# Expert tiles scattered as fp16 high and low parts and loaded by a transposing DMA, with three sets of banks and buffers and the first layer two tiles ahead

## The chip, the cores and the metric

The kernel runs on 1 core of a Trainium2 chip. The core has five engines that work side by side: TensorE (PE, matrix products), VectorE (DVE), ScalarE (ACT), GpSimd (POOL) and SyncE (SP, which here only issues DMAs). The metric is the device time of one execution in microseconds (us), here the median of 3 runs.

## The reference, cut to what matters

The program is a gated two-layer block over 32 sequences of 128 tokens with 256 features. The second part of the second layer is a mixture of 8 experts of which each token takes 2, and it is this part that the change touches:

```python
x2 = layernorm(x).reshape(T, 256)              # T = 32 * 128 = 4096 tokens
logits = x2 @ router_w                         # 8 experts
probs = softmax(logits); top_p, top_e = top_k(probs, 2)
for each of the 2 * 4096 (token, expert e) rows:
    h = gelu(x2[row] @ w_in[e] + b_in[e])      # 256 x 256
    y = (h @ w_out[e] + b_out[e]) * top_p
out = x + tanh(g_ffn[1]) * (sum of a token's two y)
```

## The kernel before, in words

**Stage 1, pairs of sequences.** 16 pairs (p = 0 to 15) go through the first layer, the attention and the router. All engines work on several pairs at once in an order written out by hand, one list of calls for each engine. At the end of a pair its attention output is added (`make_x3`), normalised ("E": `statistics_e`, `means`, `variances` on DVE, `inverse_root("E", p)` on POOL, `shifts` on DVE), and ACT writes the normalised rows twice (once for each choice) into `xn_e`, with the number of the output row in column 256 (`normed_e`, `output_rows`). PE transposes them for the router (`transpose_e`), DVE picks experts and finds each row's place (`slots`), and POOL scatters the rows with four indirect DMAs of 128 rows (`scatter`, line 765) into `store_x` in HBM, where the rows of one expert lie together. A row is 257 float32.

**Stage 2, tiles of 256 rows.** `store_x` is read back in 39 tiles (i = 0 to 38), each of one expert. SP issues `load_block(i)` (line 525), 257 KB, into one of five buffers `xb` (later 14). PE transposes a tile with four 128x128 products (`transpose_block`, line 1826) into PSUM. ACT copies it as fp16 (`copy_hi`), DVE writes the rest that fp16 lost (`copy_lo`). The first layer is 12 products (`layer1`: high by high, high by low and low by high, two halves), then ACT applies the gelu and makes the high part of the hidden values (`gelu`, `hidden_hi`), DVE the low part (`hidden_lo`). The second layer is 12 more products (`layer2`), DVE adds the bias into `y_out` (`add_bias`), and POOL scatters the two halves of the tile into `store_y` (`keep_block`, line 771, 128 rows of 1 KB each). `y_out` has five buffers. DVE's `take_rows(i)` writes the scatter's row numbers and waits until the scatter of tile i - 5 has landed. Between the two scatters of a tile POOL raises a 128x2 array to a power (`long_pause`, line 778), up to tile 35. PE's order is transposition of tile i, first layer of i - 1, second layer of i - 2. Banks and buffers of the hidden values come in two sets.

**Stage 3, sums.** SP loads the two outputs of each token (`load_outputs`), DVE adds them with the gates to x (`add_pair`), partly beside the last tiles. The last pairs need the last tile.

Each engine works strictly in the order of its list, and so does SP's queue. Around the handover from stage 1 to 2 SP's list reads: load tile 0, load tile 1, `keep_parts("q", 15)` (store the last pair's queries to scratch), `stack_queries(15)` (eight loads of them), then the other tiles. The scores of pair 15 on PE wait for these.

## Time and profile before

| | |
|---|---|
| runs | 472.47, 473.06, 476.50 us (median 473.06) |
| profiled execution | 474.49 us, of it 472.6 us span of the trace |
| busy PE / DVE / ACT / POOL | 394.9 / 368.8 / 331.4 / 268.7 us |
| DMA | 87.10 MB, mean 184 GB/s |

The profile lists for each engine how long it was busy, for groups of instructions how long the engine stood idle before them and what ended that wait, and the chain of work that ended last. Busy PE is not PE at its peak, since products overlap; the spacing of their starts tells the pace. A busy share is a mean over stages that have different bounds, so the stages are looked at one by one.

### The profile page before, as it was taken

How to read it: one execution, taken by the hardware profiler on the slowest of the kernel's cores; microseconds unless marked ns; L12 is line 12 of the kernel's file. 1: busy time of each engine (PE TensorE's matmuls, PEld its weight loads, DVE VectorE, ACT ScalarE, POOL GpSimd, SP SyncE). 2: the span in 40 equal slices, each digit the busy share in tenths (PEclk: the TensorE clock that was granted, in tenths of full speed). 3: DMA queues.
4: the chain of work that ended last, by engine and by line, in shares of the span. 5: the costliest groups of instructions: out<-in, count | busy, mean ns of one | idle time of the engine just before them, and what ended most of it. 6: DMA issues, size and time to landing. Idle time of an engine off the chain costs nothing.

```text
span 472.6 us, 13099 instructions
## 1 busy us (share of the span) xinstructions
PE 394.9 (84%) x4092; PEld 308.3 (65%) x4092; DVE 368.8 (78%) x1416; ACT 331.4 (70%) x671; POOL 268.7 (57%) x313
## 2 busy tenths in 40 slices
PE   2758899998999989999899987789559999979850
PEld 1536667776776777677686765568438897967740
DVE  2888888998988889899789786367655667779994
ACT  2855788898889889898879877566706666646640
POOL 2522112545454364626545565769988888888870
PEclk9998999999999999999999999899959999999996
DMA  7245576664565555875553774624335569396985
GB/s 242 83 139 163 180 214 179 196 181 141 177 213 170 166 171 167 221 204 184 180 174 111 223 220 121 198 68 130 101 126 143 170 175 332 116 341 251 323 275 204
DMA packets 69500, 87.10 MB, mean 184 GB/s; under 512 B 9485, under 2 KB 55290, under 8 KB 69306
## 3 DMA queue, kind: packets, MB, share of 16 engines
q1 hardware_dynamic: 60074, 65.81, 46.7%
q0 software_dynamic: 6816, 18.65, 10.8%
q10 hardware_dynamic: 2544, 1.81, 1.2%
q8 instruction: 35, 0.57, 0.5%
q14 instruction: 31, 0.25, 0.2%
HBM read 51.07 MB, written 35.18 MB: 182 GB/s over the span
## 4 chain that ended last, share of the span: by engine, by line
PE 42%; POOL 17%; issue 14%; DVE 10%; DMA 8%; ACT 6%; ACTq 0%; POOLq 0%; DVEq 0%; SPq 0%
PE ps_J L1650 12%; PE ps_F L1650 6%; POOL store_y L771 6%; DMA store_y<-y_out,y_row 6%; PE ps_O L1764 5%; PE ps_T L1659 5%; POOL store_x L765 5%; PE ps_S L1751 5%; POOL pause_t L778 5%; PE ps_R L1689 2%; PE ps_O L1775 2%; PE ps_G L1650 2%; DMA temp_t<-in_temp 1%; DVE y_out L2934 1%; DVE xb_lo L2903 1%
## 5 line engine op out<-in xcount | busy, mean ns | idle before, releaser
L771 POOL DMA_INDIRECT store_y<-y_out,y_row x78 | 81.4, 1044 | 21.8 <-issue 16.5
L765 POOL DMA_INDIRECT store_x<-xn_E,slot_u x64 | 68.0, 1063 | 26.5 <-DVE slot_u L2633 13.6
L1089 ACT ACTIVATE prob<-ps_S 128x512 f32<-128x512 f32 x128 | 72.4, 594 | 12.7 <-PE ps_S L1751 10.0
L778 POOL TENSOR_TENSOR pause_t<-half_ones,minus_half 128x2 f32<-128x2 f32 x71 | 54.7, 770 | 1.9
L1751 PE MATMUL ps_S<-q_stack,k_stack 128*128 128x256 f16 x256 | 44.5, 276 | 5.9 <-issue 3.8
L2922 DVE TENSOR_TENSOR h_lo<-h_f,h_hi 128x512 f16<-128x512 f32 x39 | 26.9, 689 | 21.0 <-ACT h_hi L1173 9.4
L1650 PE MATMUL ps_J<-wout_hi,h_hi 128*128 x112 | 31.2, 278 | 14.3 <-DVE y_out L2934 10.9
L1764 PE MATMUL ps_O<-prob,v_wide 128*32 128x128 f32 x1024 | 41.0, 279 | 1.1 <-ACT prob L1089 0.5
L1165 ACT ACTIVATE h_f<-ps_F,bin_t 128x256 f32<-128x256 f32 x56 | 23.4, 470 | 24.5 <-PE ps_F L1650 18.9
L751 POOL TENSOR_TENSOR rstd_C<-var_C,minus_half 128x2 f32<-128x2 f32 x16 | 12.1, 759 | 40.4 <-DVE var_C L2412 40.4
L1650 PE MATMUL ps_F<-xb_hi,win_hi 128*128 128x256 f16 x112 | 31.7, 283 | 3.9 <-DVE xb_lo L2903 3.3
L1751 PEld LDWEIGHTS ps_S<-q_stack,k_stack 128*128 128x128 f16 x256 | 21.7, 98 | 17.3 <-issue 10.4
L1775 PE MATMUL ps_O<-wo_t,av 128*128 128x256 f32 x128 | 31.2, 387 | 1.9 <-ACT av L1117 1.5
L1764 PEld LDWEIGHTS ps_O<-prob,v_wide 128*32 128x32 f32 x1024 | 24.2, 109 | 12.3 <-issue 10.2
L1650 PE MATMUL ps_F<-xb_lo,win_hi 128*128 128x256 f16 x112 | 31.6, 283 | 0.0
L1650 PE MATMUL ps_F<-xb_hi,win_lo 128*128 128x256 f16 x112 | 31.5, 281 | 0.0
L1650 PE MATMUL ps_J<-wout_hi,h_lo 128*128 x112 | 31.1, 278 | 0.0
L1650 PE MATMUL ps_J<-wout_lo,h_hi 128*128 x112 | 31.1, 278 | 0.0
L1152 ACT ACTIVATE xb_hi<-ps_R 128x512 f16<-128x512 f32 x28 | 16.6, 594 | 19.6 <-PE ps_R L1826 15.9
L751 POOL TENSOR_TENSOR rstd_E<-var_E,minus_half 128x2 f32<-128x2 f32 x16 | 11.8, 737 | 31.0 <-DVE var_E L2412 30.8
L756 POOL TENSOR_TENSOR inv_norm<-norm2c,minus_half 128x2 f32<-128x2 f32 x16 | 11.1, 694 | 32.2 <-DVE norm2c L2481 32.2
L1775 PEld LDWEIGHTS ps_O<-wo_t,av 128*128 128x128 f32 x128 | 23.1, 190 | 6.8 <-ACT av L1117 3.5
(301 smaller groups left out, 1399.5 us busy)
## 6 DMA issues: line engine op xcount, KB each, us to landing
parts_scratch<-parts SPq DMA_DIRECT2D x32, 256.0 KB
k_stack<-parts_scratch SPq DMA_DIRECT2D x64, 128.0 KB
q_stack<-parts_scratch SPq DMA_DIRECT2D x128, 64.0 KB
xb<-store_x SPq DMA_DIRECT2D x30, 257.0 KB
y_got<-store_y SPq DMA_DIRECT2D x14, 512.0 KB
c_in<-in_ctx SPq DMA_DIRECT2D x16, 256.0 KB
x_in<-in_x SPq DMA_DIRECT2D x16, 256.0 KB
store_x<-zeros SPq DMA_DIRECT2D x15, 257.0 KB, 4.6
```

Of the source, the lines that this page charges most:

```text
L751: pool.tensor_tensor(rstd[k][q][:, :], var[k][q][:, :], minus_half[:, 0:2], ALU.pow)\
L765: pool.indirect_dma_start(store_x, bass.IndirectOffsetOnAxis(slot_u[q][:, at:at + 1], 0), xn_e[q][:, at, :], None).then_inc(s_scat[q], 16)
L771: pool.indirect_dma_start(store_y, bass.IndirectOffsetOnAxis(y_row[n][:, b:b + 1], 0), y_out[n][:, b, :], None).then_inc(s_y_kept[n], 16)
L778: pool.tensor_tensor(pause_t[:, :], half_ones[:, :], minus_half[:, 0:2], ALU.pow).then_inc(s_set_p, 1)
L1089: act.activation(prob[m % PROBS][:, 2 * n:2 * n + 2, :, :], bank_s[n], ACT.Sigmoid, scale=float(HD) ** -0.5).then_inc(s_prob[n], 1)
L1165: act.activation(h_f32[q][:, m, :], hid_banks[side(i)][:, m, :], ACT.Gelu_apprx_tanh, bias=biases[:, bass.ds(at + m, 1)]).then_inc(s_gelu, 1)
L1650: ins = pe.matmul(o, l, r, start=start and i == 0, stop=stop and i == len(seq) - 1, skip_group_check=skip)
L1659: ins = pe.transpose(bank_t[:, i, b, :], src[:, b, 128 * i:128 * i + 128], ident[:, :])
L1751: ins = pe.matmul(bank_s[n][:, g % 2, :, :], k_stack[q][:, g, k, cut], q_stack[q][:, :, g, k, cut], start=True, stop=True)
L1764: ins = pe.matmul(bank_av[32 * g:32 * g + 32, k, b, :], v_wide[q][:, b, 4 * k + g, 2 * h:2 * h + 2, :].rearrange("p a d -> p (a d)"), prob ...
L1775: ins = pe.matmul(bank_o[:, b, :], av[:, k, b, :], wo_t[:, k, :], start=(k == 0), stop=(k == KT - 1))
L2922: dve.tensor_tensor(h_lo[q][:, :, :], h_f32[q][:, :, :], h_hi[q][:, :, :], ALU.subtract) .then_inc(s_h_lo, 1)
```

## The change

**Rows.** The row in `store_x` keeps its 1,028 bytes, but the first 1,024 now hold the 256 values as fp16 high parts and then as fp16 low parts. ACT writes the high parts (`rows_hi`, same two activations as before but fp16 out). DVE computes the normalised rows once in float32 into a separate array `xn_f` (`normed_e`, two instructions of 128x256 for each pair). POOL subtracts the one from the other and writes the low parts (`rows_lo`, one instruction of 128x1024 for each pair). `scatter(p)` waits for it. `transpose_e` reads `xn_f`.

**Tiles.** `load_block` issues a transposing DMA of 256 rows by 512 fp16 values, and a second DMA for the row numbers (256 pieces of 8 bytes). The first layer reads the landed tile directly: `transpose_block`, `copy_hi` and `copy_lo` are gone. A tile's buffer comes free after its first layer.

**Sets.** The hidden values and their PSUM banks, and the banks of the second layer, come in three sets instead of two (`HB = 3`); the first layer runs two tiles ahead of the second. The other loops are now written out as lists with the same content.

```diff
+            def rows_lo(p):
+                pool.wait_ge(s_rows_hi, 2 * p + 2)
+                pool.wait_ge(s_xn["E"], 2 * p + 2)
+                pool.tensor_tensor(e_lo[p % 2], xn_f[:, :, :].unsqueeze(2).broadcast_to([128, 2, TOP, D]), e_hi[p % 2],
+                                   ALU.subtract).then_inc(s_rows_lo, 1)
...
+            def normed_e(p):
...
+                for b in range(2):
+                    dve.tensor_scalar(xn_f[:, b, :], xs[:, 2 * p + b, :], mv["E"][q][:, b, 0:1], rstd["E"][q][:, b:b + 1],
+                                      ALU.subtract, ALU.mult).then_inc(s_xn["E"], 1)
...
-                    sp.wait_ge(s_xb_t, j + 1)
+                    sp.wait_ge(s_h, j + 1)
                     sp.wait_ge(s_y_row, j + 1)
-                sp.dma_start(xb[n][:, :, :], store_x[bass.ds(row_at(i, 0), BLK), :]
-                             .rearrange("(p b) c -> p b c", b=SUB))\
-                    .then_inc(s_xb[n] if n < XB else s_late[(n - XB) // GROUP], 16)
+                at, done = row_at(i, 0), s_xb[n] if n < XB else s_late[(n - XB) // GROUP]
+                sp.dma_start(xb[n][:, :, :], store_x16[bass.ds(at, BLK), 0:2 * D], transpose=True).then_inc(done, 16)
+                sp.dma_start(row_no[n][:, :, :], store_x[bass.ds(at, BLK), D - 1:WIDE].rearrange("(b p) c -> p b c", b=SUB))\
+                    .then_inc(done, 16)
...
-                pe.wait_ge(s_xb_lo, i + 1)
+                    loaded(pe, i)
...
-                               [(xb_hi[q][:, k, :], xb_lo[q][:, k, :]) for k in range(KT)])
+                               [(tile[:, k, :], tile[:, KT + k, :]) for k in range(KT)])
...
-        hid_banks = [P[n][:, :].rearrange("p (k s) -> p k s", k=KT) for n in ("F", "S0")]
-        y_banks = [P[n][:, :].rearrange("p (b d) -> p b d", b=SUB) for n in ("J", "S1")]
+        hid_banks = [P[n][:, :].rearrange("p (k s) -> p k s", k=KT) for n in ("F", "S0", "R")]
+        y_banks = [P[n][:, :].rearrange("p (b d) -> p b d", b=SUB) for n in ("J", "S1", "O")]
```

Three places where instructions move. First SP's list at the handover, before the change. `xb` is a tile, `parts_scratch` the stored queries, `q_stack` their eight loads.

```order
127 L525 DMA xb<-store_x 128x514
128 L525 ISA
129 L525 DMA xb<-store_x 128x514
130 L476 DMA parts_scratch<-parts 128x2x512
131 L499 DMA q_stack<-parts_scratch 16x4x512 x8
```

And after it.

```order
127 L533 DMA_TRANSPOSE xb<-store_x 128x4x256
128 L534 ISA
129 L534 DMA row_no<-store_x 128x2x2
130 L533 ISA
131 L533 DMA_TRANSPOSE xb<-store_x 128x4x256
132 L534 ISA
133 L534 DMA row_no<-store_x 128x2x2
134 L483 DMA parts_scratch<-parts 128x2x512
135 L506 DMA q_stack<-parts_scratch 16x4x512 x8
```

Four issues instead of two, two of them transposing, now stand ahead of the store of the queries.

Second, POOL's list where the first tiles' scatters meet the last pair's, before the change (`store_y` is a tile's scatter, `store_x` a pair's, `pause_t` the pause).

```order
199 L771 DMA store_y<-y_out,y_row 28160x256
200 L778 TENSOR_TENSOR pause_t<-half_ones,minus_half 128x2
201 L765 DMA store_x<-xn_E,slot_u 36608x257
202 L778 TENSOR_TENSOR pause_t<-half_ones,minus_half 128x2
203 L765 DMA store_x<-xn_E,slot_u 36608x257
```

And after it.

```order
214 L846 DMA store_y<-y_out,y_row 28160x256
215 L857 TENSOR_TENSOR pause_t<-half_ones,minus_half 128x2
216 L829 TENSOR_TENSOR xn_E<-w_f,xn_E 128x4x256
217 L840 DMA store_x<-xn_E,slot_u 36608x257
218 L857 TENSOR_TENSOR pause_t<-half_ones,minus_half 128x2
219 L840 DMA store_x<-xn_E,slot_u 36608x257
```

The subtraction (`rows_lo(15)`, printed with the names of the memory that it shares) is put between the pause and the pair's first scatter. All else keeps its place, the pauses too.

Third, DVE's list in the steady part of stage 2, before the change, one tile.

```order
1068 L2903 TENSOR_TENSOR xb_lo<-ps_R,xb_hi 128x512
1069 L2913 TENSOR_TENSOR y_row<-xb,left_rows 128x2
1070 L2922 TENSOR_TENSOR h_lo<-h_f,h_hi 128x512
1071 L2934 ISA
1072 L2934 TENSOR_TENSOR y_out<-ps_J,bout_t 128x512
```

And after it.

```order
1065 L3269 TENSOR_TENSOR y_row<-row_no,left_rows 128x2
1066 L3278 TENSOR_TENSOR h_lo<-h_f,h_hi 128x512
1067 L3290 ISA
1068 L3290 TENSOR_TENSOR y_out<-ps_J,bout_t 128x512
```

The tile's low part is gone, the other three instructions stay in their order.

## Rows read from the trace of the kernel before

**Rows 1.** Stretches of the span: us of each engine, granted clock, DMA share, GB/s.
```profile
54.00:290.00 236.00, 219.64 (x2597) 166.79 (x2589) 204.36 (x941) 201.56 (x421) 111.52 (x133) 1.00 0.61 181
341.00:461.00 120.00, 100.28 (x860) 85.11 (x860) 89.07 (x201) 64.80 (x127) 98.97 (x104) 0.96 0.67 222
461.00:472.60 11.60, 0.00 (x0) 0.00 (x0) 4.96 (x12) 0.00 (x0) 0.96 (x1) 0.60 0.59 205
```

**Rows 2.** Page part 4: the chain that ended last, by engine.
```profile
PE 42%; POOL 17%; issue 14%; DVE 10%; DMA 8%; ACT 6%; ACTq 0%; POOLq 0%; DVEq 0%; SPq 0%
```

**Rows 3.** POOL in order of time, tiles' scatters: start, us, instruction, idle before.
```profile
344.20 0.96 POOL L771 DMA_INDIRECT store_y<-y_out,y_row  x1 [0.30 <-issue]
345.18 0.73 POOL L778 TENSOR_TENSOR pause_t<-half_ones,minus_half 128x2 f32<-128x2 f32 x1
346.10 1.04 POOL L771 DMA_INDIRECT store_y<-y_out,y_row  x1 [0.19 <-issue]
347.44 0.96 POOL L771 DMA_INDIRECT store_y<-y_out,y_row  x1 [0.30 <-issue]
...
423.81 1.39 POOL L771 DMA_INDIRECT store_y<-y_out,y_row  x1 [0.20 <-issue]
...
461.11 0.96 POOL L771 DMA_INDIRECT store_y<-y_out,y_row  x1 [0.30 <-issue]
```

**Rows 4.** POOL in order of time at the handover.
```profile
310.13 1.04 POOL L765 DMA_INDIRECT store_x<-xn_E,slot_u  x1 [3.37 <-DVE slot_u L2633]
...
318.57 1.52 POOL L771 DMA_INDIRECT store_y<-y_out,y_row  x1 [0.19 <-issue]
...
340.87 1.04 POOL L771 DMA_INDIRECT store_y<-y_out,y_row  x1 [0.20 <-issue]
```

**Rows 5.** Waits from 300 us on: who for whom, us in all, times, longest.
```profile
DVE y_row L2913 <- DMA store_y<-y_out,y_row: 13.1, 8, 7.0
...
POOL store_y L771 <- DVE y_out L2934: 5.2, 11, 0.8
```

**Rows 6.** PE in order of time, one tile.
```profile
385.13 0.27 PE L1650 MATMUL ps_S<-xb_hi,win_hi 128*128 128x256 f16 x1
...
387.75 0.60 PE L1826 MATMUL ps_T<-ident,xb 128*128 128x128 f32 x4
388.18 0.27 PE L1650 MATMUL ps_F<-xb_hi,win_hi 128*128 128x256 f16 x1
```

**Rows 7.** Groups by shape: instruction, count, busy us, mean ns, idle before.
```profile
L784 POOL MEMSET v_wide<- 128x1024 f32 x2 | 1.9, 952 | 0.0
...
L2903 DVE TENSOR_TENSOR xb_lo<-ps_R,xb_hi 128x512 f16<-128x512 f32 x28 | 19.1, 682 | 1.4 <-ACT xb_hi L1152 1.4
...
L2403 DVE BATCH_NORM_STATS2 stats_E<-xs 128x6 f32<-128x256 f32 x32 | 11.9, 412 | 0.1
```

**Rows 8.** SP's queue in order of time at the handover: start, us of issuing.
```profile
287.39 0.94 SPq L525 DMA_DIRECT2D xb<-store_x  x2
288.44 0.38 SPq L476 DMA_DIRECT2D parts_scratch<-parts  x1
```

**Rows 9.** PE in order of time when pair 15's scores begin.
```profile
298.50 0.60 PE L1751 MATMUL ps_S<-q_stack,k_stack 128*128 128x256 f16 x4 [1.98 <-issue]
299.88 0.39 PE L1650 MATMUL ps_F<-xb_hi,win_hi 128*128 128x256 f16 x1 [0.78 <-DVE xb_lo L2903]
```

**Rows 10.** Page part 3: DMA queues, packets, MB, share of 16 engines.
```profile
q1 hardware_dynamic: 60074, 65.81, 46.7%
q0 software_dynamic: 6816, 18.65, 10.8%
```

**Rows 11.** Waits from 60 to 290 us.
```profile
PEld ps_T L1659 <- ACT xn_E L1026: 1.7, 2, 1.3
```

**Rows 12.** POOL in order of time, the inverse roots of pairs 1 and 14.
```profile
86.41 0.69 POOL L751 TENSOR_TENSOR rstd_E<-var_E,minus_half 128x2 f32<-128x2 f32 x1 [5.94 <-DVE var_E L2412]
...
298.08 0.72 POOL L751 TENSOR_TENSOR rstd_E<-var_E,minus_half 128x2 f32<-128x2 f32 x1 [1.40 <-DVE var_E L2412]
```

More of the change, by code:

```diff
@@ L955, in _ @@
             long_pause()
+            rows_lo(14)
             scatter(14, 3)
@@ L3218, in _ @@
             shifts("E", 1)
+            normed_e(1)
             squares(4)
@@ L3966, in _ @@
             add_bias(8)
[L3968 to L3982 removed]
+            take_rows(11)
```

767 lines of the change are left out of this document (606 added, 161 removed).

## The prediction, made before the changed kernel was run

> **What bounds the kernel now.** I read the stretches first. From 54 to 290 us (stage 1) PE is busy 219.64 of 236 us and DVE 204.36, that is 93% and 87%; POOL only 47% [rows 1]. From 341 to 461 us (stage 2) PE is at 84%, DVE at 74%, ACT at 54%, while POOL shows 98.97 of 120 us [rows 1]. By shares alone PE would be the bound of stage 2, so the order of time has to decide. On PE a tile's products start at 385.13, the transpositions of the next tile at 387.75 and the next tile's products at 388.18 [rows 6]: 24 products in 2.62 us (0.109 each) and 0.43 us for the transpositions, 3.05 us a tile. On POOL a tile is one scatter at 344.20, a pause, a second scatter at 346.10, and the next tile's at 347.44 [rows 3]: 3.24 us a tile, with gaps of 0.30 and 0.19 us that end by "issue", so in which nothing was waited for. 3.24 is more than 3.05. So POOL, not PE, sets the pace of stage 2, although its busy share counts the gaps as idle. The rest of the trace agrees. From the scatter at 344.20 (tile 4) to the last at 461.11 (tile 38) are 116.9 us. The floor is 32 tiles at 3.24, then five scatters without pauses at about 1.27: 110.0. Only 6.9 us are stalls or lengthened issues, such as the one of 1.39 us [rows 3]; waits for `y_out` are part of it, 5.2 us from 300 us on, where the ordinary 0.2 to 0.3 of each is counted in [rows 5]. The chain that ended last has 42% PE, from stage 1, and 17% POOL with 14% "issue", mostly POOL's gaps [rows 2]. Behind the last scatter 11.6 us of landing, loading and adding follow [rows 1], which the change leaves alone.
>
> At the handover POOL waits 3.37 us for the places of pair 14 until 310.13, and from there works through four scatters, the tiles 0 to 2, pair 15's four scatters and tile 3 at 340.87 [rows 4], without a wait that counts. So the end of the kernel hangs on three things: when pair 14's places come (310.1), what POOL has to do from there on, and its stalls.
>
> **The change, part by part.**
>
> *Taken off the tiles.* PE loses 0.43 us a tile [rows 6], DVE 0.68 us (`xb_lo`, [rows 7]), ACT a copy. With POOL at 3.24 us a tile this buys nothing by itself: PE goes from 3.05 to 2.62 us and waits more. What it can take away is part of the 6.9 us of stalls. The third set and the first layer two tiles ahead act in the same direction. But DVE's `take_rows` waits 13.1 us in all for tile scatters to land, up to 7.0 us at a time [rows 5], and these waits, which precede `add_bias` in DVE's order, do not depend on PE; and the issue of 1.39 us is not changed either. I take 3.0 us of the 6.9: −3.0, between 0 and −6.9.
>
> *First tile.* The first products of tile 0 waited 0.78 us for `xb_lo` [rows 9]; the landed tile is there by then: −0.8.
>
> *`rows_lo(15)`.* It stands in POOL's unbroken stretch, so it counts in full. No such instruction is in the trace. A POOL memset of the same 1,024 elements takes 0.95 us [rows 7], a bound from below since it only writes; two operands in and one out at that pace would be 2.86, my bound from above. I take the middle, +1.9. The Trainium skill (GPSIMD Engine Reference, Performance versus the Vector engine) measures a two-operand operation over 2,048 elements at 4,497 ns, by which 1,024 would be an estimate of 2.25 us, and the sum 0.35 us higher; no row of this trace shows it.
>
> *`rows_lo(0)` to `(14)`.* They stand where POOL waits: 3.37 us before pair 14's first scatter [rows 4], 5.94 and 1.40 us before inverse roots [rows 12]. Where the wait is shorter than 1.9 us the inverse root comes up to 0.5 to 2 us late, of which ACT's order has covered most. I count 0 for these. If the cover is gone, each costs up to 1.9.
>
> *`normed_e`.* 32 instructions of 128x256 on DVE. The nearest row is `stats_E` over the same elements at 0.412 us [rows 7]: 0.8 us a pair, 13.2 in all. A pair takes 16.3 us (298.08 − 86.41 over 13 pairs, [rows 12]), of which DVE works 87%, 14.1 us [rows 1]; it would work 14.9. Nothing of it shows if the idle 13% takes it, all 13.2 if none does. I take a quarter, +3.3. Against that PE no longer waits for ACT's `xn_E` (1.7 us in stage 1, [rows 11]), since DVE's rows are ready sooner. Together +1.6.
>
> *The handover on SP.* Two tile loads take 0.94 us to issue, and the store of the queries follows at 288.44 [rows 8]; pair 15's scores begin at 298.50 after a wait [rows 9], and pair 14's router and its places come behind them on PE. Four issues in place of two put the store back by at least 0.94 us. The tiles ahead in the queue may also take longer. By the hardware queue's mean a packet of 1,095 bytes takes 58.8 ns (46.7% of 16 x 472.6 us over 60,074), by the software queue's one of 2,736 bytes 119.8 ns [rows 10]. The line through both is 18 ns a packet and 0.037 ns a byte. A tile takes 0.86 us as a load at the queue's mean rate; as 1,024 pieces of 256 bytes, my estimate of what a transposition reads, 27.5 ns each on 16 engines, it would take 1.76. Two tiles make 1.8 us, of which I count half: +1.8 in all, between 0.9 and 5.
>
> Sum: −3.0 − 0.8 + 1.9 + 1.6 + 1.8 = +1.5 us on a span of 472.6, so 474.1, and an execution of 476.0 where this one took 474.49 (1.9 us lie outside the span). The runs' median is 473.06; +1.5 on it is 474.6.
>
> **The rivals.**
>
> *A: POOL stays the bound (as above).* Ends of the unknown terms: −6.9, −0.8, +1.0, −1.7, +0.9 give −7.5; 0, 0, +2.9, +13.2, +5 give +21. They will not all fall one way; I give this case 467 to 480. Chance 0.60.
>
> *B: the transposing load is slower than a tile's 3.24 us.* If pieces are written 32 bytes at a time, a tile is 8,192 pieces, which at 18 to 19 ns are 9.9 us on 16 engines [rows 10]. It decides from 3.24 us a tile on. At 5 us the 39 tiles issued from 287.4 land at 482 instead of before 435, and with the 20 to 30 us that follow a last load the end is near 510. Against it: nothing in the trace forces pieces that small. The Trainium skill (DMA: Bandwidth & Descriptors, Latency and other measured facts) measured 261 GB/s for transposing DMAs, an estimate of 1.0 us for 256 KB; by that case B is out, and no row here shows it. Chance 0.15.
>
> *C: stage 1 becomes bound by DVE.* If DVE stands still while POOL subtracts, a pair's DVE time is 14.1 + 0.8 + 1.9 = 16.8 us against 16.3: +0.5 for each of 15 pairs and the waits of an engine without slack, some +8 to +15, 481 to 488. It decides once DVE is held for more than 1.4 us a pair. For it speaks that POOL's issues lengthen from 1.04 to 1.39 us in the late stretch in which DVE adds outputs [rows 3], so the two engines do seem to disturb each other. The Trainium skill (SBUF — State Buffer, SBUF: two separate sides) has a rule for it: DVE with two operands in SBUF and POOL share an exclusive lock for the whole instruction; by that rule only such DVE work is held, about a third of it. Chance 0.12.
>
> *D: faster by more than 1%.* The mechanism is the stall on POOL: if all 6.9 us were waits that shorter DVE and PE work removes, and stage 1 hides its additions, −6.9 − 0.8 + 1.0 + 0.9 = −5.8, 467.3. It needs a gain of 4.7 us or more. A gain like PE's 0.43 us x 39 = 17 us is excluded as long as POOL needs 3.24 us a tile. Chance 0.13.
>
> **How the numbers follow.** The likeliest is A, 474.6. 1% is 4.7 us and about what a measurement can tell. Same (468.3 to 477.8): 0.45 of A's 0.60 and 0.02 of C's. Slower: 0.13 of A, 0.15 of B, 0.10 of C. Faster: 0.02 of A and 0.13 of D. The range 467 to 488 leaves out B and a small part of the others.
>
> **What would show it.** POOL's tile period stays at 3.24 to 3.4 us while PE's 24 products take 2.62 and PE idles more: right. `rows_lo` at 1 to 2.9 us, with pair 15's between scatters: right. The store of the queries on SP about 1 us later. I am wrong if PE waits for loads of tiles (B), if a pair takes over 16.8 us (C), or if POOL's period falls under 3.2 us.

## The result and the profile after

The changed kernel takes 511.61 us (median, 507.63 to 513.64), beside 473.15 of the kernel before on the same chip: 1.079 times the time, with an interval of 1.070 to 1.087. The prediction was 474.6, the range 467 to 488. Both were wrong, and so was the weight on "same". In e9 and in e12 one run each was over 1.5% above the fastest run of its kernel; these two are left out of the ratios below.

| | before | after |
|---|---|---|
| span of the profiled execution | 472.6 us | 511.8 us |
| busy PE / DVE | 394.9 / 368.8 us | 392.5 / 379.3 us |
| busy ACT / POOL | 331.4 / 268.7 us | 309.2 / 305.7 us |
| packets of the hardware queue | 60,074 | 106,250 |

The first lines are from the page of the kernel after, parts 1, 3 and 4. The chain that ended last was PE's for 42% [rows 2]; now it is POOL's for 31%, and DVE's share is 17% where it was 10%.

```profile
PE 392.5 (77%) x3936; PEld 298.5 (58%) x3936; DVE 379.3 (74%) x1409; ACT 309.2 (60%) x632; POOL 305.7 (60%) x329
...
q1 hardware_dynamic: 106250, 65.86, 49.7%
...
POOL 31%; PE 21%; DVE 17%; issue 17%; ACT 7%; DMA 6%; POOLq 1%; ACTq 0%; DVEq 0%; SPq 0%
```

The stretches of [rows 1] in the kernel after (us of PE, PE's weight loads, DVE, ACT, POOL, then the granted clock, DMA share, GB/s). In the same 236 us of stage 1 PE does 210.35 us of work where it did 219.64, while DVE shows more, 212.61 for 204.36, in fewer instructions (880 for 941). Part of that is the work of `normed_e`; the rest is instructions that take longer than they did. In the stretch of the tiles the granted clock is 0.91 where it was 0.96, but that is not what the tiles lose: in e5 and e6, whose tiles are as quick as before in the table below, it is 0.93 and 0.92.

```profile
54.00:290.00 236.00, 210.35 (x2404) 158.54 (x2407) 212.61 (x880) 188.61 (x393) 126.85 (x134) 0.98 0.57 168
...
341.00:461.00 120.00, 84.67 (x699) 68.47 (x698) 58.93 (x152) 47.21 (x94) 95.73 (x99) 0.91 0.71 162
```

**Where the time went.** POOL in order of time (start, us, instruction, idle before) has four landmarks, which answer to [rows 12], [rows 4] and the end of [rows 3]: pair 15's inverse root, the first scatter of tile 0, the first scatter of tile 3, the last scatter.

```profile
87.81 0.69 POOL L819 TENSOR_TENSOR rstd_E<-var_E,minus_half 128x2 f32<-128x2 f32 x1 [5.16 <-DVE var_E L2763]
...
344.46 0.72 POOL L819 TENSOR_TENSOR rstd_E<-var_E,minus_half 128x2 f32<-128x2 f32 x1
345.38 1.04 POOL L846 DMA_INDIRECT store_y<-y_out,y_row  x1 [0.20 <-issue]
...
374.13 1.04 POOL L846 DMA_INDIRECT store_y<-y_out,y_row  x1 [0.20 <-issue]
...
500.36 0.96 POOL L846 DMA_INDIRECT store_y<-y_out,y_row  x1 [0.30 <-issue]
```

In the kernel before pair 15's root starts at 317.65; the others are 318.57, 340.87 and 461.11. So the span can be cut into four parts (they add up but for the 0.92 us between pair 15's root and tile 0's first scatter, the same in every run), and the same four can be read in every experiment:

| us | pair 15's root | tile 0 to tile 3 | tile 3 to last | last to end | span |
|---|---|---|---|---|---|
| before | 317.65 | 22.30 | 120.24 | 11.5 | 472.6 |
| after | 344.46 (+26.8) | 28.75 (+6.5) | 126.23 (+6.0) | 11.4 | 511.8 |
| e1 subtraction small | 319.84 | 27.05 | 125.66 | 11.7 | 485.2 |
| e2 `normed_e` small | 338.94 | 28.72 | 126.47 | 11.8 | 506.8 |
| e3 both small | 319.42 | 26.88 | 126.05 | 11.6 | 484.9 |
| e4 subtraction on DVE | 337.97 | 27.23 | 126.50 | 11.8 | 504.4 |
| e5 plain load | 343.84 | 29.08 | 120.65 | 12.0 | 506.5 |
| e6 no pauses | 347.62 | 27.67 | 120.93 | 11.9 | 509.0 |
| e7 before, no pauses | 320.33 | 20.28 | 125.68 | 12.1 | 479.3 |
| e8 before, busy POOL | 329.21 | 23.79 | 121.37 | 12.2 | 487.5 |
| e9 outputs earlier | 345.77 | 28.54 | 122.78 | 12.7 | 510.7 |
| e10 queries first | 342.97 | 28.62 | 126.20 | 11.4 | 510.1 |
| e11 subtraction in four | 342.90 | 29.63 | 124.07 | 11.6 | 509.1 |
| e16 plain, transposition later | 342.46 | 24.36 | 121.33 | 11.7 | 500.8 |
| e17 plain, three mends | 337.77 | 24.63 | 121.96 | 11.8 | 497.1 |
| e18 as e17, subtraction small | 320.79 | 24.62 | 120.90 | 12.0 | 479.2 |

The 39.2 us are three losses at three places, 26.8 in stage 1, 6.5 at the handover and 6.0 in the steady tiles. The experiments find a main cause for each.

A column of one profiled execution also moves from run to run without a cause. Pair 15's root does so most: the edits of e6, e9 and e10 come into play only after it or beside it, and it is at 347.6, 345.8 and 343.0, where the changed kernel has 344.5; in e7 it is 2.7 us later than in the kernel before. So up to some 5 us in the first column mean nothing by themselves. The third column of these kernels without an edit in stage 2 (after, e1 to e4, e10) lies between 125.7 and 126.5. Verdicts on a whole kernel are taken from the ratios. The kernel before, timed beside each of the four groups of experiments, took 473.0, 476.9, 477.8 and 471.6 us, so only ratios compare between groups (e1 to e4, e5 to e8, e9 to e12, e16 to e18).

### The profile page after: what moved, and what is told of

Same layout as the page of the kernel before. It is cut to its first block, busy times and chain, and to the rows that moved or that the text cites. A ratio compares the mean times of both kernels' runs of the same rounds, so it can differ in the third digit from the quotient of the medians.

```text
span 511.8 us, 12756 instructions
## 1 busy us (share of the span) xinstructions
PE 392.5 (77%) x3936; PEld 298.5 (58%) x3936; DVE 379.3 (74%) x1409; ACT 309.2 (60%) x632; POOL 305.7 (60%) x329
## 3 DMA queue, kind: packets, MB, share of 16 engines
q1 hardware_dynamic: 106250, 65.86, 49.7%
## 4 chain that ended last, share of the span: by engine, by line
POOL 31%; PE 21%; DVE 17%; issue 17%; ACT 7%; DMA 6%; POOLq 1%; ACTq 0%; DVEq 0%; SPq 0%
POOL store_y L846 11%; POOL pause_t L857 8%; POOL store_x L840 7%; PE ps_J L1891 5%; PE ps_T L1900 3%; DMA store_y<-y_out,y_row 3%; PE ps_O L2005 2%; PE ps_F L1891 2%; POOL xn_E L829 2%; PE ps_S L1891 2%; DMA y_got<-store_y 2%; POOL rstd_E L819 1%; ACT xn_B L1218 1%; PE ps_S L1992 1%; PE ps_R L1930 1%
## 5 line engine op out<-in xcount | busy, mean ns | idle before, releaser
L846 POOL DMA_INDIRECT store_y<-y_out,y_row x78 | 83.7, 1073 | 28.4 <-issue 17.6
L1285 ACT ACTIVATE prob<-ps_S 128x512 f32<-128x512 f32 x128 | 72.4, 594 | 24.6 <-PE ps_S L1992 23.6
L840 POOL DMA_INDIRECT store_x<-xn_E,slot_u x64 | 69.2, 1081 | 29.8 <-DVE slot_u L2996 19.0
L1354 ACT ACTIVATE h_f<-ps_S,bin_t 128x256 f32<-128x256 f32 x26 | 10.9, 471 | 41.9 <-PE ps_S L1891 37.4
L829 POOL TENSOR_TENSOR xn_E<-w_f,xn_E 128x1024 f16<-128x1024 f32 x16 | 33.1, 2068 | 0.3
L819 POOL TENSOR_TENSOR rstd_C<-var_C,minus_half 128x2 f32<-128x2 f32 x16 | 12.2, 760 | 35.2 <-DVE var_C L2763 35.1
L2005 PEld LDWEIGHTS ps_O<-prob,v_wide 128*32 128x32 f32 x1024 | 24.6, 110 | 12.6 <-issue 9.3
L1891 PE MATMUL ps_S<-wout_hi,h_hi 128*128 x52 | 15.7, 302 | 19.4 <-DVE h_lo L3278 19.3
L1249 ACT ACTIVATE xn_E<-xs,shift_E,rstd_E 128x512 f16<-128x512 f32 x32 | 24.2, 808 | 9.9 <-DVE shift_E L2769 9.9
L3278 DVE TENSOR_TENSOR h_lo<-h_f,h_hi 128x512 f16<-128x512 f32 x39 | 26.8, 688 | 2.1 <-ACT h_hi L1362 2.1
L1354 ACT ACTIVATE h_f<-ps_R,bin_t 128x256 f32<-128x256 f32 x26 | 10.9, 470 | 28.9 <-PE ps_R L1891 27.1
L1362 ACT ACTIVATE h_hi<-h_f 128x512 f16<-128x512 f32 x39 | 24.6, 630 | 1.2
L1280 ACT ACTIVATE parts<-ps_J 128x512 f16<-128x512 f32 x32 | 19.0, 594 | 10.0 <-PE ps_J L1891 9.9
L819 POOL TENSOR_TENSOR rstd_E<-var_E,minus_half 128x2 f32<-128x2 f32 x16 | 11.8, 738 | 22.1 <-DVE var_E L2763 21.7
L2825 DVE TENSOR_TENSOR parts<-ps_J,parts 128x512 f16<-128x512 f32 x32 | 21.9, 684 | 4.2 <-ACT parts L1280 4.1
```

Source lines behind the costliest of these rows:

```text
L819: pool.tensor_tensor(rstd[k][q][:, :], var[k][q][:, :], minus_half[:, 0:2], ALU.pow)\
L829: pool.tensor_tensor(e_lo[p % 2], xn_f[:, :, :].unsqueeze(2).broadcast_to([128, 2, TOP, D]), e_hi[p % 2], ALU.subtract).then_inc(s_rows_lo, 1)
L840: pool.indirect_dma_start(store_x, bass.IndirectOffsetOnAxis(slot_u[q][:, at:at + 1], 0), xn_e[q][:, at, :], None).then_inc(s_scat[q], 16)
L846: pool.indirect_dma_start(store_y, bass.IndirectOffsetOnAxis(y_row[n][:, b:b + 1], 0), y_out[n][:, b, :], None).then_inc(s_y_kept[n], 16)
L1285: act.activation(prob[m % PROBS][:, 2 * n:2 * n + 2, :, :], bank_s[n], ACT.Sigmoid, scale=float(HD) ** -0.5).then_inc(s_prob[n], 1)
L1362: act.activation(h_hi[q][:, :, :], h_f32[q][:, :, :], ACT.Copy).then_inc(s_h_hi, 1)
```

## The experiments

The theories after the result. **H (hold):** DVE stands still while POOL subtracts, in far more cases than rival C had it. **W (work):** the additional work of `normed_e` on a nearly full DVE is the loss. **B:** the transposing load. **P (pace):** POOL's list in stage 2, pauses and all, is what everything waits for. Later: **S**, SP's issues come late, and **O**, an order on PE.

### e1, e2, e3: the two additions cut down, one by one and together

In e1 and e3 POOL subtracts one column, in e2 and e3 DVE normalises eight:

```diff
-pool.tensor_tensor(e_lo[p % 2], xn_f[:, :, :]..., e_hi[p % 2], ALU.subtract)
+pool.tensor_tensor(e_lo[p % 2][:, :, :, 0:1], xn_f[:, :, 0:1]..., e_hi[p % 2][:, :, :, 0:1], ALU.subtract)
...
-dve.tensor_scalar(xn_f[:, b, :], xs[:, 2 * p + b, :], ...)
+dve.tensor_scalar(xn_f[:, b, 0:8], xs[:, 2 * p + b, 0:8], ...)
```

> The changed kernel with POOL's rows_lo cut to 1 of 256 values per row (the low parts of the scattered rows stay zero, so they are left out of the result); all waits stay. Theory H (DVE is held while POOL's subtraction runs): in the changed kernel's trace DVE's picks take 594 ns instead of 187, var_E 553 instead of 173, the two at which the subtraction usually falls; all together some 1.7 us a pair. They go back to 187 and 173, the pair period falls from 18.1 us to about 16.9, and the kernel to about 490 us (15 pairs x 1.2 = 18, and 2 for the one subtraction in POOL's unbroken stretch). Rival W (DVE's own new work, 0.82 us a pair, is what slows stage 1): the period stays at 17.8 or more and the time above 503 us.

Measured: 487.95 us, ratio 1.031 (1.022 to 1.039).

> The changed kernel with DVE's normed_e cut to 8 of 256 values (the router and the low parts see wrong rows; this work is left out); rows_lo in full. Theory H: only 0.5 us of DVE work a pair goes, the stretched instructions stay at 594 and 553 ns, the period falls from 18.1 to 17.4 to 17.7, the kernel to 500 to 505 us. Rival W: the period goes back to 16.3 to 16.6 and the kernel to about 487 us.

Measured: 508.03 us, ratio 1.073 (1.065 to 1.081), slower than the 500 to 505 that H had said, though a pair takes 17.66 us, as said.

> Both cuts at once (low parts and float32 rows left out, all waits and places kept). Theories H and W both: the period is back at 16.3 to 16.5 us and stage 1 costs nothing, so the time is what is left of the loss outside stage 1: handover 4 us and stage 2 with its transposing loads 6 us over the kernel before, 483 to 487 us. If a third cause in stage 1 exists (the order PE waits in, or DMA), the period stays above 16.8 us and the time above 490.

Measured: 486.24 us, ratio 1.027 (1.020 to 1.035).

The subtraction costs 1.079 − 1.031, some 23 us. The work of `normed_e` costs some 3 us by e2 and 1.7 by e3 against e1, both inside the intervals. In e1 pair 15's root comes at 319.84, so 24.6 of the 26.8 us of stage 1 are back, at once. W is out.

How a subtraction on POOL gets at stage 1 is seen where DVE and POOL stand side by side in time. The kernel after, DVE in order of time at pair 14's statistics:

```profile
321.18 0.25 DVE L2759 BATCH_NORM_AGGREGATE mv_E<-stats_E 128x2 f32<-128x6 f32 x2
321.47 1.72 DVE L2763 TENSOR_SCALAR var_E<-mv_E 128x2 f32<-128x2 f32 x1
```

And POOL at the same time:

```profile
321.08 2.07 POOL L829 TENSOR_TENSOR xn_E<-w_f,xn_E 128x1024 f16<-128x1024 f32 x1
323.27 0.72 POOL L819 TENSOR_TENSOR rstd_E<-var_E,minus_half 128x2 f32<-128x2 f32 x1
```

`var_E`, two numbers per partition, 0.16 us elsewhere, begins at 321.47 and ends at 323.19; the subtraction ends at 323.15. The hold also falls on the instruction for which POOL's own next one waits.

How often does this happen? Between 54 and 290 us POOL subtracts 11 times, and in 9 of them one instruction of DVE is drawn out and does not end before the subtraction does: `x` twice, `picks` three times, `var_E` twice, `both` and `win_lo` once each. Together they take 17.1 us more than they take otherwise, 1.55 for each of the 11. The longest, DVE and then POOL:

```profile
210.98 3.13 DVE L3332 TENSOR_TENSOR win_lo<-w_stage,win_hi 128x512 f16<-128x512 f32 x1
```

```profile
211.47 2.07 POOL L829 TENSOR_TENSOR xn_E<-w_f,xn_E 128x1024 f16<-128x1024 f32 x1
```

The other two subtractions (at 101.48 and 155.67) ran beside statistics and instructions with an operand in PSUM, which kept their ordinary lengths (only a small `ln_gain` behind the first of them took 0.2 us more). The means of the groups show the same. DVE's groups by shape (count, busy us, mean ns, idle before), the kernel before:

```profile
L2448 DVE TENSOR_TENSOR x<-moved,x_in 128x512 f32<-128x512 f32 x12 | 8.1, 679 | 0.0
L2976 DVE TENSOR_TENSOR win_lo<-w_stage,win_hi 128x512 f16<-128x512 f32 x6 | 4.1, 683 | 0.0
L2412 DVE TENSOR_SCALAR var_E<-mv_E 128x2 f32<-128x2 f32 x14 | 2.4, 174 | 0.0
L2597 DVE TENSOR_TENSOR picks<-route,rindex 128x32 f32<-128x32 f32 x13 | 2.4, 186 | 0.1
L2611 DVE TENSOR_TENSOR both<-picks 128x16 f16<-128x16 f32 x13 | 2.2, 168 | 0.1
```

The kernel after:

```profile
L2799 DVE TENSOR_TENSOR x<-moved,x_in 128x512 f32<-128x512 f32 x12 | 10.6, 883 | 0.0
L2819 DVE TENSOR_SCALAR w_f<-xs,mv_E,rstd_E 128x256 f32<-128x256 f32 x24 | 8.8, 411 | 0.0
L2807 DVE TENSOR_TENSOR xt_lo_E<-ps_T,xt_hi_E 128x512 f16<-128x512 f32 x12 | 8.2, 683 | 2.0 <-issue 1.7 <-ACT xt_hi_E L1211 0.2
L2960 DVE TENSOR_TENSOR picks<-route,rindex 128x32 f32<-128x32 f32 x12 | 7.1, 594 | 0.1
L2763 DVE TENSOR_SCALAR var_E<-mv_E 128x2 f32<-128x2 f32 x12 | 6.6, 553 | 0.0
L3332 DVE TENSOR_TENSOR win_lo<-w_stage,win_hi 128x512 f16<-128x512 f32 x5 | 5.8, 1166 | 0.0
L2974 DVE TENSOR_TENSOR both<-picks 128x16 f16<-128x16 f32 x12 | 4.6, 381 | 0.0
```

And e1:

```profile
L2765 DVE TENSOR_SCALAR var_E<-mv_E 128x2 f32<-128x2 f32 x14 | 2.9, 206 | 0.0
L2962 DVE TENSOR_TENSOR picks<-route,rindex 128x32 f32<-128x32 f32 x13 | 2.4, 187 | 0.1
```

Five groups grew. Each has one instruction a pair (`win_lo` in 5 pairs of 12), and the means rose by 0.41 us for `picks`, 0.38 for `var_E`, 0.21 for `both`, 0.20 for `x`, 0.48 x 5/12 = 0.20 for `win_lo`. That is 1.40 us a pair, 68% of the 2.07 us of the subtraction (counted by subtractions it is the 1.55, 75%). `xt_lo_E`, which has one operand in PSUM (`ps_T`), did not grow, 0.683 us. The Trainium skill (SBUF — State Buffer, Who interferes with whom) has this rule: a DVE instruction with two inputs in SBUF and a GpSimd instruction that reads SBUF shut each other out, and so do GpSimd and a DVE instruction in one of the two-port modes that a `tensor_scalar` can enter; a DVE instruction with at most one SBUF input outside these modes is free; the one that starts first keeps the ports for its whole instruction. Which groups grew (`var_E`, the `tensor_scalar`, at 0.553 us for 0.174) and that `xt_lo_E` did not (0.683) agree with it. Who starts first agrees for 4 of the 9 only. The other 5, as `win_lo` above, began 0.25 to 0.60 us ahead of the subtraction and still lasted to its end.

What comes of it for the pace can be told from the roots of pair 1 and pair 14, 13 pairs apart: 16.28 us a pair before [rows 12], and (323.27 − 87.81) / 13 = 18.11 after, with pair 14's root at 323.27 in the rows of POOL above. By the same two roots a pair takes 16.25 us in e1 and 17.66 in e2. So `normed_e`'s 0.82 us alone cost nothing a pair (e1), the hold with hardly any of it 1.38 (e2), and on top of the hold `normed_e` costs another 0.45.

One rival is left. POOL's next inverse root stands directly behind the subtraction in its list, so it could be POOL's own 2 us, and not the hold, by which DVE is late. But then DVE would wait for the root. It does not. DVE's waits for it between 54 and 290 us, in the kernel before, after and in e8 below (us in all, times, longest):

```profile
DVE shift_E L2418 <- POOL rstd_E L751: 0.5, 1, 0.5
...
DVE shift_E L2769 <- POOL rstd_E L819: 0.4, 2, 0.2
...
DVE shift_E L2443 <- POOL rstd_E L752: 0.4, 2, 0.2
```

### e8: the hold alone, put into the kernel before

```diff
+pool.tensor_tensor(unread[...], zeros[...], zeros[...], ALU.subtract)   # 128x736, once a pair, where rows_lo stands
```

> The kernel before plus one idle subtraction of 128x736 float32 values for each pair on POOL, at the places where the changed kernel has rows_lo (about 1.5 us each; nothing reads its result, nothing on DVE is added). Theory H: DVE is held for most of it, picks and var_E lengthen by 0.3 us or more, the pair period rises from 16.3 to 16.9 to 17.4, and the kernel takes 483 to 490 us. Rival W: POOL had room, so 473 to 476 us.

Measured: ratio 1.029 (1.022 to 1.035), so +13.6 us on 473. DVE's groups by shape in e8, and POOL's instruction that holds them:

```profile
L2622 DVE TENSOR_TENSOR picks<-route,rindex 128x32 f32<-128x32 f32 x12 | 5.2, 432 | 0.1
L2437 DVE TENSOR_SCALAR var_E<-mv_E 128x2 f32<-128x2 f32 x13 | 5.0, 387 | 0.0
```

```profile
L764 POOL TENSOR_TENSOR unread<-zeros 128x736 f16<-128x736 f32 x12 | 17.0, 1418 | 0.3
```

Nothing reads what POOL writes here, and no other part of the change is in this kernel. 1.42 us a pair on POOL, on an engine that stands idle for half of stage 1 [rows 1], still slow the kernel; the root of pair 15 comes 11.6 us later. The first 11 of these subtractions behind 54 us hold the same nine DVE instructions as in the kernel after, for 10.8 us in all or 0.98 for each of the 11, and a pair takes 17.26 us in place of 16.28, which is 0.98 more. With the waits for the root as small as shown above, this shows H by itself. (`picks` and `var_E` grew by 0.25 and 0.21 on the mean, a little less than the 0.3 expected.)

### e4, e11: the same subtraction elsewhere, and in pieces

In e4 DVE does it (`rows_lo` as five calls after `normed_e` in DVE's list). In e11 POOL does it in four instructions:

```diff
+for b in range(2):
+    for k in range(TOP):
+        pool.tensor_tensor(e_lo[p % 2][:, b, k, :], xn_f[:, b, :], e_hi[p % 2][:, b, k, :], ALU.subtract)
```

> The changed kernel with the same subtraction on DVE (128x1024, five calls after normed_e in its list) instead of on POOL. Theory H: DVE gets 1.1 us of work a pair and loses 1.7 us of standing still, the period falls from 18.1 to about 17.5 and the kernel to 500 to 504 us although DVE does more. Rival W: more DVE work makes it slower, 520 us or more.

Measured: 505.39 us, ratio 1.068 (1.059 to 1.076), a little above the 500 to 504 expected. DVE takes 1.23 us for it (mean of 12), a pair takes 17.41 us, and the kernel is about 1% faster than with 2.07 us on POOL (the two intervals overlap). Adding work to DVE did not make the kernel slower, as W had it: 1.23 us of work of its own are no dearer here than being held for 1.40.

> The changed kernel, with POOL's subtraction of a pair cut into four of 128x256 with the same result. Theory W (DVE is kept out for the whole of one POOL instruction, and gets in between two): an instruction of DVE is held by 0.6 us at most and not by up to 1.6, and 5 to 15 us of the 39 come back, 497 to 507 us, though POOL itself takes longer for the pair (about 0.2 us for each further instruction, 2.7 against 2.07 us). Theory T (what DVE loses goes with the time in which POOL works, however it is cut): nothing comes back, and POOL's longer time makes it 512 to 520.

Measured: ratio 1.069 (1.066 to 1.073), some 4.5 us less than the 1.079 of the changed kernel, by the middles of the two intervals (they overlap slightly; that of e10, 1.079 in the same group, does not reach it). DVE's groups by shape in e11, and POOL's pieces:

```profile
L2765 DVE TENSOR_SCALAR var_E<-mv_E 128x2 f32<-128x2 f32 x12 | 8.6, 718 | 0.0
L2962 DVE TENSOR_TENSOR picks<-route,rindex 128x32 f32<-128x32 f32 x12 | 5.5, 454 | 0.1
L2976 DVE TENSOR_TENSOR both<-picks 128x16 f16<-128x16 f32 x12 | 2.4, 200 | 0.0
```

```profile
L831 POOL TENSOR_TENSOR xn_E<-w_f,xn_E 128x256 f16<-128x256 f32 x44 | 28.6, 682 | 0.3
```

Four pieces of 0.68 us take 2.5 us from the start of the first to the end of the last, in place of 2.07. `both` is nearly free again and `picks` is held less, but `var_E` more. In the order of time of e11, DVE and then POOL:

```profile
233.70 2.31 DVE L2765 TENSOR_SCALAR var_E<-mv_E 128x2 f32<-128x2 f32 x1
```

```profile
233.50 2.49 POOL L831 TENSOR_TENSOR xn_E<-w_f,xn_E 128x256 f16<-128x256 f32 x4
236.10 0.72 POOL L819 TENSOR_TENSOR rstd_E<-var_E,minus_half 128x2 f32<-128x2 f32 x1
```

`var_E` begins in the first of the four pieces and ends at 236.01, with the last. So the expectation that DVE gets in between two pieces, and is never held by more than 0.6, is wrong for this instruction; why the next piece goes first was not found. Cutting helps a little and does not cure. Where it helps is open: pair 15's root in e11 is no earlier than in e10 (342.9 and 343.0).

### e5: the load without its transposition

```diff
-sp.dma_start(xb[n][:, :, :], store_x16[bass.ds(at, BLK), 0:2 * D], transpose=True)
+sp.dma_start(xb[n]..., store_x16[bass.ds(at, BLK), 0:2 * D].rearrange("(p b) c -> p b c", b=SUB))
```

> The changed kernel with a plain load of the same bytes in place of the transposing one (256 KB, 128 partitions of 2 KB), so that the first layer multiplies untransposed rows; the row number load stays. Theory S (SP's queue is what stage 2 lost: a transposing load takes 1.23 us to issue against 0.33 to 0.47 for a plain one, so the last 14 loads take 31 us and the first output loads leave at 451 instead of 413): the first output loads leave 10 us or more earlier against the last tile scatter, POOL's stall of 4.1 us near tile 28 goes, the handover is 1.5 us shorter, and the kernel is 4 to 8 us faster, 504 to 508 us. Rival T (the transposition moves data slowly and the landing is what is late): DMA share in stage 2 falls clearly (0.71 to under 0.6) and the gain is over 10 us. Rival N: POOL hides all of it, 510 to 512 us.

Measured: ratio 1.069 (1.060 to 1.078). B's 510 us was near the measured time, but its mechanism is out. Stage 1 and the handover are as slow as with the transposition (343.84 and 29.08), and only the steady tiles lose 5.6 us of their excess. The plain load changes both the transfer and SP's time to issue it. e9 leaves the transfer as it is and gets 3.4 of the 5.6 back by SP's order alone; the other 2.1 are not told apart.

### e9: SP comes late to the outputs

SP in order of time in the kernel after, the last loads of tiles and the first of outputs (start, us of issuing):

```profile
449.19 1.23 SPq L533 DMA_TRANSPOSE xb<-store_x  x1
450.62 0.42 SPq L534 DMA_DIRECT2D row_no<-store_x  x1
451.23 3.10 SPq L546 DMA_DIRECT2D y_got<-store_y  x5
```

DVE and then POOL, a little later in the same kernel:

```profile
455.85 0.88 DVE L3306 SCALAR_TENSOR_TENSOR result<-y_got,gate_all,xs 128x256 f32<-128x256 f32 x2 [6.33 <-DMA y_got<-store_y]
```

```profile
459.07 0.96 POOL L846 DMA_INDIRECT store_y<-y_out,y_row  x1 [4.10 <-DVE y_out L3290]
```

A transposing load occupies SP for 1.23 us (0.55 in e5) and the row numbers for 0.42 more; with gaps a tile takes SP 2.0 us, and the last 14 loads (tiles 25 to 38) keep it at work almost without a gap from 419.8 to 451.0. The first outputs stand behind them; the kernel before issues these at 412.6. DVE waits 6.33 us for these with `y_out` of the next tile behind it, and POOL waits for that. In e9 they are issued ahead of the last three tiles:

```diff
             load_block(35)
+            load_outputs(0) ... load_outputs(4)
             load_block(36)
```

> The changed kernel with one edit on SP's queue: the first five loads of output rows (y_got) are issued after the load of tile 35 and not after that of tile 38. In the changed kernel DVE stands 6.33 us for the first y_got and POOL then 4.10 and 1.37 us for DVE's y_out, because SP, at 2.0 us a tile, comes to the output loads only at 451.2 us. Theory S (SP's issues are the reason of these waits): the waits go, and 3 to 5.5 us with them: 506 to 508.5 us where before is 473 and after 511.6. Rival (the tile that y_got waits for, or the landing of the scatters, is what is late): under 1 us, 510.5 to 512.

Measured: ratio 1.067 (1.063 to 1.072), about 5 us less than the changed kernel, and clear of e10 in the same group (1.074 to 1.084). The steady tiles take 122.78 us for 126.23; DVE's wait for the outputs falls from 6.3 to 2.8 us, and POOL's waits for `y_out` in the tiles from 6.3 to 3.7. The outputs leave only 2.6 us earlier (448.6 for 451.2). S holds for this place, though e12 below does not repeat the gain.

### e10: the queries' store ahead of the first tiles

```diff
+            keep_parts("q", 15)
             load_block(0)
             load_block(1)
-            keep_parts("q", 15)
             stack_queries(15)
```

> The changed kernel with one edit on SP's queue: the store of the last pair's queries is issued ahead of the loads of tiles 0 and 1, and not behind them. Theory S: the store goes 3.6 us earlier and the eight loads of the queries start about 2.3 us earlier, so that PE's wait for them (4.71 us) shrinks by as much; 1.5 to 2.5 us fall: 509 to 510. Rival: PE's later wait (4.61 us for the transposition of pair 15, whose rstd stands behind pair 14's scatters on POOL) swallows it: 511 to 512, no change.

Measured: ratio 1.079 (1.074 to 1.084), no change. The eight loads start at 316.38 and not at 318.31, but PE waits 4.62 us later on all the same, as the rival said. What the prediction had costed as the handover on SP is not what the handover loses.

### e16: the order on PE at the handover

PE in order of time in the kernel after, with the transposition of pair 15's rows and the second layer of tile 1 (`ps_S`) behind it:

```profile
346.12 1.12 PE L1900 MATMUL ps_T<-ident,w_f 128*128 128x128 f32 x4 [4.61 <-DVE w_f L2819]
...
349.59 0.42 PE L1891 MATMUL ps_S<-wout_hi,h_hi 128*128 x1
```

POOL, which waits for tile 1 and then for tile 2:

```profile
352.85 1.04 POOL L846 DMA_INDIRECT store_y<-y_out,y_row  x1 [3.60 <-DVE y_out L3290]
...
357.55 1.04 POOL L846 DMA_INDIRECT store_y<-y_out,y_row  x1 [0.92 <-DVE y_out L3290]
```

In the kernel before this transposition stood behind the second layer of tile 1 on PE, in the one after ahead of it. It needs DVE's rows, these POOL's root of pair 15, and the root stands behind pair 14's four scatters. So tile 1 now waits for pair 15. This order is measured on the kernel with the plain load only, not with the transposing one. e16 puts it back, on the kernel of e5, so its tiles stand wrongly as in e5:

```diff
-            transpose_e(("E", 14), 15)
             layer1(3, 0)
             layer1(3, 1)
             layer2(1, 0)
             layer2(1, 1)
+            transpose_e(("E", 14), 15)
-            logits(("rank", 14), 15)
             layer1(4, 0)
             layer1(4, 1)
+            logits(("rank", 14), 15)
```

> The kernel of e5 (changed kernel, tiles loaded without transposition, so that the columns of a tile stand wrongly and its output is not the reference's) with one edit on PE's list: the transposition of pair 15's rows for the router stands behind the second layer of tile 1, as in the kernel before, and not ahead of it. In e5 the second layer of tile 1 stands behind it and POOL then waits 3.91 and 0.92 us for y_out; from tile 0's first scatter to tile 3's it takes 29.08 us, in the kernel before 22.30. Theory O (the new place in PE's list is what the handover loses): POOL's 3.91 goes, the 29.08 becomes 24 to 26.5, and 2.5 to 5 us fall: 502 to 504.5 where before is 473 and e5 506.5. Rival (the path runs through pair 15's router to its scatters, whichever product stands first): under 1 us.

Measured: 502.20 us, ratio 1.064 (1.058 to 1.069). By the ratios alone that is 2.7 us under e5, inside their intervals. But the second column, which moved by 0.2 us only between the changed kernel, e2, e9 and e10, is plain. POOL in order of time in e16, tile 0 and tile 3:

```profile
343.38 1.04 POOL L847 DMA_INDIRECT store_y<-y_out,y_row  x1 [0.20 <-issue]
...
367.74 1.04 POOL L847 DMA_INDIRECT store_y<-y_out,y_row  x1 [0.20 <-issue]
```

24.36 us for 29.08, POOL's waits of 3.91 and 0.92 are gone, and so are 4.7 of the 6.8 us that e5 had lost there. 2.1 us stay, and their cause was not settled.

### e12, e17, e18: the causes together

> The changed kernel with both edits of SP's queue (outputs earlier, queries first) and with POOL's subtraction cut to one of 256 columns, so that the low parts of the rows are left out: what is left of the cost of the change when DVE is not held and SP is not late. The same kernel without the edits of SP gave 487.95 (ratio 1.031). Theory (hold, SP's late output loads, and SP's late queries make up the loss but for PE's wait at the handover): 479 to 483 us. Rival (there is a gain of the change hidden under these costs): 473 or less. Rival (SP's queue was not what cost): 486 to 488.

Measured: ratio 1.028 (1.023 to 1.033), against 1.031 for e1, so the two edits of SP bring nothing that these intervals can tell. The expectation of 479 to 483 was too low, and with the subtraction small the 5 us of e9 are not seen again. So what the late outputs cost is shown for the changed kernel as it stands and not as a fixed price. Its profiled execution is left out of the table, since it does not stand for the median (495.1 us of span).

e17 is e16 with the outputs earlier and the subtraction in four; e18 is e16 with the outputs earlier and the subtraction of one column.

> The kernel of e16 (tiles loaded without transposition, output not the reference's) with outputs loaded earlier on SP and POOL's subtraction in four instructions as well. In e5 SP was not late any more, so that two causes are mended here: the place of the transposition (2.5 to 5 us) and part of the hold (4.5). If they add: 497 to 500 us where before is 473 (ratio 1.051 to 1.057). If both end in the same wait: 502 to 504.

Measured: 497.80 us, ratio 1.053 (1.048 to 1.057).

> The kernel of e16 (tiles loaded without transposition) with outputs loaded earlier and POOL's subtraction cut to one of 256 columns, so that the low parts of the rows are left out too: none of the three named costs is left. Theory (hold of DVE, SP's issues, place of the transposition: these are the loss): 475 to 479 us where before is 473. Rival (tiles that need no transposition on PE are worth something once the rest is mended): 470 or less. Rival (something not yet named costs 10 us in stage 2): 483 or more.

Measured: 479.58 us, ratio 1.015 (1.011 to 1.019).

The gains add: 1.069, 1.064, 1.053 in the order e5, e16, e17 (the first step is inside the intervals, the second is clear of them). In e18 none of the three causes is left, and 1.5% of 7.9 remain, just above the 475 to 479 expected: 3.1 us in stage 1, which is within what that column moves by itself, 2.3 at the handover, 0.7 in the tiles. It also speaks to whether the change hides a gain: with the three mended and the load plain, the steady tiles take 120.90 us, as before (120.24). No version tried beats the kernel before.

### e6, e7: the pauses between a tile's scatters taken out

The pause between the two scatters of a tile is left out, on the changed kernel (e6) and the one before (e7).

> The changed kernel without POOL's pauses between the two scatters of a tile (36 of 0.73 us with their gaps of 0.19). Theory P (POOL's 3.24 us a tile sets the pace of stage 2): a tile takes about 2.7 us, and stage 2 gets 10 to 18 us shorter, 494 to 502 us. Rival: the pace is set by the landing of the scatters or by DVE's takes of rows, and the pauses' 33 us turn into waits: 508 us or more.

Measured: ratio 1.071 (1.062 to 1.079), 506 to 507 us on 473 and not the 494 to 502 of P. The 33 us of pauses mostly turn into waits: in the tiles POOL waits 30.7 us for `y_out` where the changed kernel waits 6.3. Even so the steady tiles take 120.93 us for 126.23. So the 6.0 us that they had lost come back here without an edit of SP's queue, and late outputs are not the only thing by which they can be mended.

> The kernel before without the same pauses. Theory P: POOL goes to 2.5 us a tile, PE with 3.05 us becomes the bound, so stage 2 gains 0.2 us x 36 = 7 us at most and less what DVE and the landings take: 466 to 471 us. Rival (POOL was not the bound): 472 to 474 us, no change. With e6 it tells what the removal of PE's transpositions is worth once POOL does not hide it.

Measured: ratio 1.016 (1.008 to 1.024): slower where P said 466 to 471 us, with 0.7 us of POOL less in every tile.

e7's largest wait of POOL from tile 0's scatter to the last (who for whom, us, times, longest), and POOL in order of time:

```profile
POOL store_y L771 <- DVE y_out L2928: 39.3, 24, 4.3
```

```profile
366.70 0.96 POOL L771 DMA_INDIRECT store_y<-y_out,y_row  x1 [2.34 <-DVE y_out L2928]
...
374.28 0.96 POOL L771 DMA_INDIRECT store_y<-y_out,y_row  x1 [2.34 <-DVE y_out L2928]
```

POOL now waits 39.3 us where it waited 5.2 [rows 5]. Here tiles come in twos, 7.58 us for two, 3.79 each, where the kernel with pauses made 3.24; from 439 us on a tile takes 3.45, with DVE at work for 27.5 of the 28 us up to the last scatter. So P is wrong as a theory of what a faster POOL would bring. POOL does set 3.24 us a tile, but the other engines have little more than that in hand, and in this kernel, without the pauses, they fall into a rhythm that is worse. Why into this one was not settled.

## Why the prediction was wrong, point by point

**`rows_lo(0)` to `(14)` at nothing: this step failed, and it is the largest error.** It asked what waits for POOL's instruction and found cover in POOL's waits. What it left out is what the instruction does to its neighbour: 1.40 us of DVE a pair, on an engine that works 87% of stage 1. With it go some 23 of the 39 us (e1), 15 x 1.40 = 21 of them by the mean of a pair.

**Rival C was the mechanism, at under a third of its size and a chance of 0.12.** It compared sums, 16.8 us of DVE work with a pair of 16.3, and got +0.5 a pair; the measured one is +1.83. The failing term is the idea that DVE's 13% of idle time absorbs the hold first. It absorbs `normed_e` when that comes alone (16.25 us a pair in e1), and it does not absorb a hold: 1.38 us a pair for 1.40 in e2, 0.98 for 0.98 in e8. Why work is absorbed and a hold is not was not tested. A likely reason is that DVE's gaps are waits for other engines (9.0 us between 54 and 290 us for `xs`, which waits for PE), and that these wait for DVE in turn. The +8 to +15 was reached by adding "the waits of an engine without slack" without a row. The share was misread, too. "About a third" of DVE's work, the prediction says, can be held; it gives no rows for it, and it took from the rule the half on two inputs in SBUF alone, while `var_E` is held with one. But what counts is whether one such instruction comes up within the 2 us: one did in 9 of 11 subtractions, and 68 to 75% of the subtraction's time was lost.

**`rows_lo`'s duration:** 1.9 forecast, 2.07 measured, right. The estimate from the Trainium skill's page was 2.25, above the measured value. **`rows_lo(15)` in POOL's unbroken stretch, +1.9:** wrong place. That stretch had a wait by then (1.19 us for pair 15's places, 2.05 in e1 where the subtraction is small), so it costs 0 to 1.7 us: 28.75 against 27.05 in e1, and nothing in e16 against e18.

**`normed_e`, +1.6:** duration right (0.411 for 0.412). e1 still has it and is 2.2 us late at pair 15's root; e3 against e1 is 1.7 us in the times and 0.4 at the root. Right within what can be told, as long as DVE is not held; with the hold it costs 0.45 us a pair and 5.5 at the root (e2), the latter little more than that column moves by itself.

**First tile, −0.8:** the first products of tile 0 wait 0.40 us in the kernel after (for nothing that the profile shows) where they waited 0.78. They stand behind pair 15's scores, which come 25.9 us later than before, so the term could not show in the time.

**The handover on SP, +1.8:** the loss at the handover is 6.5, but not on SP (e10: nothing). The prediction had the rows of PE's wait for `xn_E` and read the transposition as something that would be ready sooner. It did not look at where `transpose_e(15)` went in PE's list, which costs 4.7 us. The order was to be had before the run.

**Tiles, −3.0:** came out as +6.0. Mechanism wrong at both ends. The stalls did not yield to the work taken off PE, ACT and DVE: 120.65 to 121.33 us in e5, e18 and e16, which leave the transposition of the tiles out altogether, 120.24 before. And the sum had no term for SP's steady work: 1.23 + 0.42 us a tile on the queue that also carries the outputs. The waits of the kernel after, from 285 us on, show what "POOL sets the pace" means: DVE, with less to do, waits longer for scatters to land, 45.6 us where it was 13.1 [rows 5].

```profile
DVE y_row L3269 <- DMA store_y<-y_out,y_row: 45.6, 20, 6.2
...
POOL store_y L846 <- DVE y_out L3290: 10.8, 7, 4.1
```

**What held:** POOL's period of 3.24 us where nothing disturbs it (393.71 to 396.95 and 407.30 to 410.54 in the kernel after), no gain from PE's 0.43 us a tile, B's transfer not the bound (0.86 and 1.76 us were both estimates under 3.24; with 1,028 bytes a row the first is 0.88), the last 11.5 us unchanged. That B's 510 us lie so near the 511.6 is luck. The Trainium skill (Advanced Engine Details and Errata, X-Bar Transpose (TRN2)) says that transposing DMAs are as fast as plain ones. No run times a single transfer. For the kernel's time nothing contradicts it: e9 is within the interval of e5 (1.067 and 1.069). The time of the DMA engines does not agree: the hardware queue's packets take 49.7% of 511.8 us in the kernel after and 46.0% of 506.5 in e5, 254.4 and 233.0 us of all 16 engines, which by an estimate is 0.55 us more for each of the 39 loads. On SP's queue the two are not alike either, 1.23 against 0.55 us.

## What to carry to other kernels

When work goes to an idle engine, price what it does to its neighbour as well as where it waits: take the other engine's instructions that can collide, see whether one of them comes up within the new instruction's length, and charge the hold in full if that engine is nearly full (here DVE at 87% paid 1.38 us for a hold of 1.40). Compare the instruction order at each handover before predicting; a transposition one place earlier tied tile 1 to the last pair. And count issues per queue in the steady state, since a queue that has time for its loads can still be late for what stands behind them.
